# Gathers on GpSimd: each begins on the signal of the one ahead, with no clearing in between

## What is computed

```python
e = jnp.stack([tbl_0[ids[:, 0]], ..., tbl_49[ids[:, 49]]], axis=1)      # 512 x 50 x 16
gram = jnp.einsum('bid,bjd->bij', e, e)
z = gram[:, _I_IDX, _J_IDX]                                             # pairs i < j
h = jnp.concatenate([z, dense_ctx], axis=1)                             # 512 x 1241
h = jnp.maximum(h @ W_top1 + b_top1, 0.0)                               # 512
h = jnp.maximum(h @ W_top2 + b_top2, 0.0)                               # 256
y = h @ W_top3                                                          # 1
```

## Time and profile before

| | us |
|---|---|
| three runs, median (lowest, highest) | 159.24 (158.18, 159.63) |
| the profiled execution | 159.45 |
| its span in the profile | 157.3 |
| TensorE busy | 127.8 (81%) |
| GpSimd busy | 124.7 (79%) |
| VectorE busy | 110.6 (70%) |
| ScalarE busy | 44.4 (28%) |

### The profile page before, as it was taken

One profiled execution on the slowest core, in us unless ns is written; L12 is line 12 of the kernel. 1 busy time (PEld: TensorE's weight loads), 2 busy tenths in 40 slices (PEclk: granted clock), 3 DMA queues, 4 the chain that ended last, 5 costly groups with the idle time before them and its releaser, 6 DMA issues.

```text
span 157.3 us, 3325 instructions
## 1 busy us (share of the span) xinstructions
PE 127.8 (81%) x1323; PEld 111.9 (71%) x1323; DVE 110.6 (70%) x193; ACT 44.4 (28%) x77; POOL 124.7 (79%) x184
## 2 busy tenths in 40 slices
PE   0007875937698999999999989999995994999992
PEld 0007764827588679978959989886695983899991
DVE  1807899998899989998898894999953019344021
ACT  8930000232205220332071205204422018444020
POOL 2989898898998989899889889898988898982000
PEclk9999998696899999999999999999999999999998
DMA  3199999734380010000000100010000000000000
GB/s 84 35 358 419 442 417 317 279 116 119 125 256 15 6 6 4 10 7 4 10 6 4 10 4 6 11 10 6 4 10 6 4 10 4 10 6 6 0 0 1
DMA packets 6486, 12.40 MB, mean 79 GB/s; under 512 B 2077, under 2 KB 5414, under 8 KB 6342
## 3 DMA queue, kind: packets, MB, share of 16 engines
q1 hardware_dynamic: 3592, 11.46, 19.7%
q0 software_dynamic: 2880, 0.74, 5.6%
HBM read 12.17 MB, written 0.03 MB: 78 GB/s over the span
## 4 chain that ended last, share of the span: by engine, by line
POOL 70%; PE 14%; issue 9%; DMA 3%; ACT 2%; DVE 1%; DVEq 0%
POOL moving L294 50%; POOL spacer L300 20%; PE psm L818 4%; PE gram L811 4%; DMA moving<-tbl,ids_sb 2%; PE gram L818 2%; PE p L818 2%; DMA ids_sb<-in_ids 1%; PE gram L792 1%; PE pt L878 1%; ACT blocks L214 1%; DVE mcols L542 1%; ACT scols L344 0%; PE pt L868 0%; DVE h2w L604 0%
## 5 line engine op out<-in xcount | busy, mean ns | idle before, releaser
L294 POOL DMA_INDIRECT moving<-tbl,ids_sb x90 | 89.3, 992 | 17.4 <-issue 14.6
L777 PE MATMUL psm<-table,onehot 128*128 128x160 f32 x208 | 36.7, 326 | 19.3 <-DVE onehot L510 12.8
L777 PEld LDWEIGHTS psm<-table,onehot 128*128 128x128 f32 x208 | 32.2, 206 | 22.3 <-issue 12.8
L818 PE MATMUL p<-z,w_sb 128*128 128x128 f32 x312 | 39.3, 276 | 2.3 <-DVE z L225 2.3
L818 PEld LDWEIGHTS p<-z,w_sb 128*128 128x128 f32 x312 | 37.1, 192 | 3.6 <-ACT z L225 1.8
L300 POOL MEMSET spacer<- 128x288 f32 x90 | 35.4, 394 | 0.0
L498 DVE TENSOR_TENSOR picked<-psm,mask 128x480 f32<-128x480 f32 (+1 forms) x36 | 22.1, 634 | 4.5 <-PE psm L777 4.2
L214 ACT COPY blocks<-mcols 32x384 f32<-32x384 f32 (+3 forms) x20 | 15.4, 771 | 32.4 <-DVE mcols L542 21.2
L220 DVE COPY z<-gram 63x384 f32<-63x384 f32 (+1 forms) x20 | 9.6, 480 | 17.3 <-PE gram L811 14.0
L482 DVE TENSOR_REDUCE fixed<-picked 128x48 f32<-128x480 f32 (+1 forms) x36 | 21.3, 627 | 0.2
L767 PE MATMUL psm<-large_table,large_hot 125*128 125x400 f32 x48 | 16.9, 501 | 0.0
(11 more groups left out here) (50 smaller groups left out, 86.5 us busy)
## 6 DMA issues: line engine op xcount, KB each, us to landing
wide<-quotients SPq DMA_DIRECT2D x4, 896.0 KB, 8.2
w_sb<-in_w SPq DMA_DIRECT2D x1, 3072.0 KB, 17.4
large_table<-tbl SPq DMA_DIRECT2D x2, 781.2 KB
moving<-tbl,ids_sb POOLq DMA_INDIRECT x90, 2.8
table<-in_small SPq DMA_DIRECT2D x1, 720.0 KB, 7.2
table<-in_small SPq DMA_DIRECT2D x1, 640.0 KB, 8.7
w_sb<-in_w SPq DMA_DIRECT2D x1, 512.0 KB
table<-in_small SPq DMA_DIRECT2D x1, 480.0 KB, 5.9
```

Of the source, the lines that this page charges most:

```text
L294: nc.gpsimd.indirect_dma_start(moving[:, t, slot, 0:D], None, table, bass.IndirectOffsetOnAxis(ap=ids_sb[:, t, field:field + 1], axis=0),) ...
L777: ins = nc.tensor.matmul(psm[:, m % 2, (f - a) * R * D:(f - a + 1) * R * D], onehot[:, t % 2, f, :], table[:, f, :], start=True, stop=True)
L818: return nc.tensor.matmul(hidden_sums(t, k), w1_sb[:, c, P * k:P * (k + 1)], z[:, t % 2, c, :], start=first, stop=last)
```

## The change

`gather` no longer clears `spacer`, which is gone with its size and the semaphore `spaced`. The indirect DMA gets a second semaphore, `described`, to which GpSimd adds 1 when it has finished the instruction, with the descriptors written and the DMA started. After each gather GpSimd waits until `described` has reached the number of gathers so far, so the next gather (and, after the last one, the end of the program) stands behind that wait. The signals of the landed data and all that waits for them are as they were.

```diff
-SPACE = 288
...
-        spacer = sb("spacer", [P, SPACE])
...
-        spaced = sem("spaced")
+        described = sem("described")
...
-            ticks = [0]
+            written = [0]
 
             def gather(t, slot, table, field, landed):
 
                 nc.gpsimd.indirect_dma_start(
                     moving[:, t, slot, 0:D], None, table,
-                    bass.IndirectOffsetOnAxis(ap=ids_sb[:, t, field:field + 1], axis=0),
+                    bass.IndirectOffsetOnAxis(ap=ids_sb[:, t, field:field + 1], axis=0), engine_sem=described,
                 ).then_inc(landed, 16)
-                if ticks[0]:
-                    pool.wait_ge(spaced, ticks[0])
-                nc.gpsimd.memset(spacer[:], 0.0).then_inc(spaced, 1)
-                ticks[0] += 1
+                written[0] += 1
+                pool.wait_ge(described, written[0])
...
-            pool.wait_ge(spaced, TILES * NL - sum(SELECTED))
```

## The result

| | before | after |
|---|---|---|
| median of the runs, us (lowest, highest) | 158.8 (158.18, 159.63) | 154.46 (153.99, 158.2) |
| profiled execution, us | 159.45 | 153.99 |
| its span, us | 157.3 | 152.2 |
| VectorE busy, us | 110.6 | 105.0 |
| GpSimd busy, us | 124.7 | 88.6 |

The ratio after / before is 0.971, with a 95% interval of 0.964 to 0.978. The forecast was 157.7 us; the gain is 2.9% and not 1%. A second measurement of both, side by side on one chip, gave 155.39 (six runs) against 158.75 (eleven), ratio 0.9778 (0.9749 to 0.9807). A chip has a faster and a slower state: medians are of all executions, ratios and intervals of those in the faster state alone.

The account below looks back on a forecast made before the run. GpSimd's gather chain ended last, but gathers were judged really late only at the last tile, TensorE covering the middle. 159.45 - 1.50 (tail) = 157.95, with the runs' median 0.21 lower: 157.7 us, range 156.0 to 166.0.

Parts of the forecast that it names:

- The tail: Last tile's first product: no longer late through the 80th gather, then bound by ScalarE's relu and copies; 1.50 us gained.
- VectorE's side of the change: VectorE operations beside GpSimd's: clearings gone but gathers denser, about even; taken as 0, between -1.6 and +1.6 us.
- rival 3: VectorE's comparisons also lose their waits for GpSimd: 1.6 us more gained, 156.1 us; chance 0.12.
- the middle: Between 33 and 121 us: TensorE covers the faster gathers, so they were costed at nothing.
- The pace: GpSimd's period from gather to gather: 1.22 us (0.95 + 0.27 for the semaphore) instead of 1.47, bounded by 1.12 and 1.44.
- Rival 1: Between gathers: the signal comes late, period 1.51 us or more, and the kernel is slower, priced at 164.1 us; chance 0.28.
- rival 4: Between gathers: the signal comes only with the landed data, period 2.57 us, total 243 us; chance 0.03.
- forecast limit of 124.4: Latest start, in us, of the 80th gather (last tile's middle group) at which the 1.50 us is still gained.
- Rival 2: Before 58 us: denser gathers holding VectorE, or one more low-clock TensorE product, cost 1.3 us: 159.0 us; chance 0.17.

Follow-up runs that it names:

- plain: The changed kernel without the wait between gathers; the signal is waited for once, at the program's end: 155.42 us, ratio 0.979.
- after_third: The changed kernel once more, unaltered, on an ordinary chip, side by side with one without the wait: 155.39 us, ratio 0.9778.
- paced: The changed kernel with two semaphore hops of GpSimd to itself behind each gather, to space gathers without clearings: 187.8 us, ratio 1.1685.
- clear_tiny: The kernel before the change with clearings of 1 column, not 288; clearings and their semaphore stay: 155.85 us, ratio 0.9795.

## Why the prediction was wrong

The side it took was right, the size was not: 1.5 us forecast, 3.4 to 4.3 by the two pairs of medians. The tail, the only term of the sum, came nearly as forecast. The failed step is the term that was set to nothing.

**VectorE's side of the change** ("Clearings gone, gathers denser: about even, between -1.6 and +1.6 us. I take 0"). It was set from one row: the subtraction at 27.53 that ends together with the gather beside it, read as "a gather holds VectorE as a clearing does". A gather can hold such a small operation, and does so in the changed kernel too, but the large ones hardly pay for gathers. Without clearings the comparisons last 789 to 803 ns on the mean, whether gathers are 1.27 or 1.87 us apart; with them 917. The page's 10.4 us of comparisons fell to 8.9, so clearings made 1.5 of the 1.6 us that the prediction had found, as rival 3 said. (That the 1.6 came out is partly luck: twelve times the shortest, 0.735, took no notice of eight of the twelve being larger, 811 ns against 750 in the changed kernel.) And the copies, 3.1 us, were in no term and no rival, since only the comparisons' line had been read for its spread.

Of the 4.6 us, what lies in the later tiles is hidden by TensorE (the middle: 0.00), and what lies before 50 us is not. There the clearings cost 1.5 us by the profiles, between 1.2 and 1.8, once load and clock are taken out. So the term stands near the end of its own bounds. The other ways in which the sum was short were in no term: 0.28 us behind the last tile's first product, some 0.3 us around the span, 0.13 in the tail. By the medians of the second measurement 3.05 us of the gain are span (156.6 to 153.55) and 3.05 - 1.63 - 0.28 = 1.1 us are left for the first 50 us; in the first measurement about 2.1. The profiles' 3.19 holds 0.72 of earlier load and 0.82 of a product at a higher clock, which differs from profile to profile of one kernel.

The Trainium skill (SBUF — State Buffer, Who interferes with whom) has the rule that sorts these rows: copies and operations with a scalar can enter the modes in which VectorE takes the port pair it shares with GpSimd, multiplications of two tensors and reductions can't. The trace agrees: 917 to 790 and 613 to 459 ns for the former, 634 to 632 and 627 to 626 for the latter. The same page (A bandwidth-pool intuition that's wrong) gives about 3100 ns for a DMA whose descriptors GpSimd writes, when it is locked out behind such a copy, against 620 alone; here no gather's row exceeds 1.51 us in the changed kernel or 1.56 in any run, against 0.94, so the measurement decides for a small price on GpSimd's side. The port pair is the page's account: the runs show which operations are longer, not where the two engines meet. Why clearings of 144 columns cost the copies nothing stays open.

**The pace.** Forecast 0.95 + 0.27 = 1.22 us, measured 0.94 + 0.30. The value was right for a wrong reason: the 0.27 was taken as the price of a wait, but plain has 0.30 without one. The 0.17 of the earlier trace rows holds only behind a clearing. Rival 1 (the signal comes late) is refuted by the same rows, and rival 4 by the same 1.25 us against a shortest landing of 2.2.

**The tail.** Forecast 1.50, measured 1.63 in the changed kernel: the copies start 0.11 us before the recorded end of ScalarE's relu, not 0.03 behind it. That ScalarE and not the gather decides is shown by holding that gather back: at 117.70 nothing is lost, at 126.76 3.50 us. The forecast limit of 124.4 for its start lies between; the runs place it no nearer. In every profile with the 80th gather in time, with clearings or without, the stretch from the third tile's second product is 13.2 to 13.3 us (before 14.94).

**The middle.** Costed at nothing, measured 0.00 of 68 us.

**Rival 2** (the 1.5 us given back early by a product at the low clock). Its event does occur: the first product takes 3.33 us before and 2.5 to 3.6 us without clearings. In four profiles with full clearings somewhere it took 3.2 to 3.4 us, so whether it is quick more seldom with them is not shown. Without them it came and went in one and the same kernel (2.51 in after, 3.60 in after_third), so it gives back nothing by rule; it is up to 1.1 us of chance in any one profile.

## What to carry to other kernels

When an instruction on GpSimd goes, look at every kind of VectorE operation that stands beside it and compare the mean with the shortest of its kind and size: copies within SBUF and operations with a scalar can be paying for it, and only those in a stretch where VectorE feeds the bound will give time back. A wait of 7.7 us is worth what the next-latest input of its consumer leaves, here 1.5. And on another chip the kernels without the filler that costs 2 to 3% here took 27 to 36% longer than the one with it: time such a change on more than one.

## What the runs showed of the hardware that was not expected

- Two indirect DMAs in a row on GpSimd stand 0.30 us apart with or without a wait for the first one's signal; behind a clearing of 288 or 144 columns the gap is 0.17, of one column 0.19.
- GpSimd signalling itself twice makes that gap 0.90 us (paced).
- A clearing of 128 x 288 floats takes 0.35 us; taking 90 of them away shortens VectorE's comparisons by 14% and its copies within SBUF by 25%, while gathers 1.29 or 1.87 us apart make no difference (790, 795 ns). Clearings of 144 columns (0.23 us) cost the copies nothing (462 ns).
- Copies out of PSUM, multiplications by a mask and sums are the same with and without clearings (480, 634 to 632, 627 to 626 ns).
- On two chips TensorE and VectorE stall while gathers run 1.26 to 1.40 us apart, with one matmul every 2 to 3 us, and kernels take 241 to 251 us instead of 145 to 156. One of six runs of clear_tiny on an ordinary chip took 266 us too. What is blocked, and whether the distance or the clearing prevents it, stays open.
